# Recurrent attention and gated feed-forward on one Trainium2 core: normalisation steps spread over the score pass, norms stored ahead of the row maxima

## The reference

```python
x = L0_attn_x
xn = _layernorm(x, axis=-1)
s = _L0_attn_ref(xn, L0_attn_Wq, L0_attn_Wk, L0_attn_Wv, L0_attn_Wo)
g = _silu(_L0_ffn_ref(xn, L0_ffn_w_fc, L0_ffn_w_proj))
x = x + s * g
...
scores = jnp.einsum('bhqd,bhkd->bhqk', q, k) / math.sqrt(dk)
scores = jnp.where(causal[None, None], scores, -jnp.inf)
attn = jax.nn.softmax(scores, axis=-1)
```

## Time and profile before

| what | value |
|---|---|
| time, median of 3 runs | 1205.97 us (1204.27 to 1207.26) |
| profiled execution, its time | 1208.05 us |
| profiled execution, its span | 1206.2 us |
| TensorE busy | 1157.1 us, 96% of the span |
| VectorE busy | 851.2 us, 71% |
| ScalarE busy | 787.0 us, 65% |
| GpSimd busy | 522.0 us, 43% |
| mean granted TensorE clock | 0.995 |

### The profile page before, as it was taken

The page is one execution under the profiler, slowest core; times in us unless marked ns, Lnnn a source line. Parts: engine busy times, 40 slices in busy tenths (PEclk is TensorE's granted clock), DMA queues, the critical chain, the costliest instruction groups (busy, mean ns, idle before and its releaser), DMA issues.

```text
span 1206.2 us, 19952 instructions
## 1 busy us (share of the span) xinstructions
PE 1157.1 (96%) x7580; PEld 562.3 (47%) x7580; DVE 851.2 (71%) x1445; ACT 787.0 (65%) x1486; POOL 522.0 (43%) x894
## 2 busy tenths in 40 slices
PE   4989999999999999999899999999989999999997
PEld 3555544445444454445444454444534445444553
DVE  7988948697457975588446985569735797557864
ACT  3687974487825977269561797438873487816974
POOL 2135361463525544363343635246352463526434
PEclk9999999999999999999899999999999999999999
DMA  8390011900137000550007401091011900146010
GB/s 296 149 117 26 1 28 50 161 19 2 28 39 136 19 4 26 78 115 1 26 4 85 108 2 29 1 155 38 3 28 17 158 19 2 27 55 95 9 38 36
DMA packets 52537, 67.30 MB, mean 56 GB/s; under 512 B 9304, under 2 KB 34264, under 8 KB 51928
## 3 DMA queue, kind: packets, MB, share of 16 engines
q1 hardware_dynamic: 52440, 66.01, 29.0%
HBM read 31.98 MB, written 8.40 MB: 33 GB/s over the span
## 4 chain that ended last, share of the span: by engine, by line
PE 60%; DVE 20%; ACT 15%; DMA 3%; issue 1%; SPq 1%; DVEq 0%; ACTq 0%
PE banks L378 24%; PE banks L524 9%; PE banks L493 9%; ACT banks L778 8%; PE banks L609 5%; PE banks L578 5%; DVE mix L1025 4%; ACT arena L799 4%; DVE arena L1049 4%; DVE arena L1047 4%; PE banks L472 2%; DMA stacks<-mix 2%; DVE banks L1033 1%; PE banks L399 1%; DVE mix L1039 1%; DVE mix L928 1%
## 5 line engine op out<-in xcount | busy, mean ns | idle before, releaser
L524 PE MATMUL banks<-projT,arena 128*128 128x512 f16 x1024 | 293.7, 380 | 0.0
L778 ACT ACTIVATE banks<-banks,mix,scl 128x512 f32<-128x512 f32 (+2 forms) x384 | 250.1, 698 | 4.5 <-POOL mix L1218 2.2
L1025 DVE TENSOR_REDUCE mix<-banks 128x1 f32<-128x384 f32 (+3 forms) x352 | 221.1, 639 | 28.7 <-PE banks L479 15.6
L493 PE MATMUL banks<-xT,fcT 128*128 128x512 f16 x1024 | 227.7, 379 | 0.1
L799 ACT ACTIVATE arena<-banks,scl 128x1280 f32<-128x1280 f32 x128 | 164.7, 1328 | 72.4 <-PE banks L578 69.3
L1211 POOL TENSOR_TENSOR xh_buf<-xh_buf 128x512 f32<-128x512 f32 x120 | 152.3, 1269 | 90.7 <-ACT xh_buf L747 86.5
L1202 POOL TENSOR_TENSOR split_buf<-xr_buf,split_buf 128x512 f16<-128x512 f32 x64 | 74.0, 1178 | 238.8 <-ACT split_buf L724 238.8
L378 PE MATMUL banks<-xT,qkT 128*128 128x512 f16 x768 | 168.7, 379 | 0.0
L1218 POOL TENSOR_SCALAR mix<-mix,scl 128x1 f32<-128x1 f32 (+1 forms) x288 | 76.3, 265 | 182.9 <-DVE mix L1025 182.3
L493 PEld LDWEIGHTS banks<-xT,fcT 128*128 128x128 f16 x1024 | 97.7, 98 | 120.1 <-ACT xh_buf L747 8.0
L1232 POOL TENSOR_SCALAR_AFFINE_SELECT arena<-arena 128x256 f32<-128x256 f32 x256 | 102.7, 428 | 90.0 <-ACT arena L799 90.0
(11 more groups left out here) (148 smaller groups left out, 1563.7 us busy)
## 6 DMA issues: line engine op xcount, KB each, us to landing
stacks<-split_buf SPq DMA_DIRECT2D x192, 128.0 KB, 5.5
xr_buf<-in_L_attn_x_dram SPq DMA_DIRECT2D x8, 1024.0 KB, 7.6
out_dram<-arena SPq DMA_DIRECT2D x32, 256.0 KB, 2.3
resid<-in_L_attn_x_dram SPq DMA_DIRECT2D x28, 256.0 KB, 6.8
stacks<-in_L_ffn_w_fc_dram SPq DMA_DIRECT2D x1, 4096.0 KB, 27.1
arena<-in_L_ffn_w_proj_dram SPq DMA_DIRECT2D x1, 4096.0 KB, 14.6
mix<-norm_row SPq DMA_DIRECT2D x8, 256.0 KB, 4.6
v_sb<-in_L_attn_Wv_dram SPq DMA_DIRECT2D x1, 1024.0 KB, 8.2
```

Of the source, the lines that this page charges most:

```text
L493: mm = pe.matmul(banks[:, UP_BANKS[f % NUB], :], fcT[:, c, f * P:(f + 1) * P], xT[:, part, c, :], start=(c == 0 and part == 0), stop=(c == ...
L524: mm = pe.matmul(banks[:, 6 + t % 2, :], lhs, projT[:, f, :], **ends)
L778: mm = nc.scalar.activation(block, block, ACT.Exp, scale=col(EXP_SCALE), bias=exp_bias[:, i, h0 + k:h0 + k + 1], accum_out=row_sum[:, i, h ...
L1025: nc.vector.tensor_reduce(row_max[:, i, h0:h0 + n], scores_of(r), AX_X, ALU.max).then_inc(max_ready, 1)
```

## The change

GpSimd's `normalise` becomes a generator, `normalise_steps`, that pauses after each of its ten operations. In the first score pass one operation is issued ahead of each bias from round 8 on, so they stand ahead of the biases of rounds 8 to 17. The operations themselves and their semaphores are the same. Of SyncE's `spread_norms` the four norm stores become a function of their own, `store_norms`, and are written ahead of the wait for `maxT_ready`, so ahead of the maxima transfer. The read back stays behind it.

```diff
+NORM_FROM = 8
...
+            def store_norms(b):
+
+                sp.wait_ge(ln_ready, b + 1)
+                for t in range(NT):
+                    sp.dma_start(norm_row[t * P:(t + 1) * P], norm_c[:, t:t + 1]).then_inc(row_dma, 16)
+
             def spread_norms(b, first=False):
 
-                sp.wait_ge(ln_ready, b + 1)
-                for t in range(NT):
-                    sp.dma_start(norm_row[t * P:(t + 1) * P], norm_c[:, t:t + 1]).then_inc(row_dma, 16)
                 sp.wait_ge(row_dma, b * NT * 16 + NT * 16)
...
+                if not last:
+                    store_norms(b + 1)
                 sp.wait_ge(maxT_ready, b + 1)
                 sp.dma_start(q_stack[KS:KM, :, :], maxT[:, :]).then_inc(max_dma, 16)
                 if not last:
                     spread_norms(b + 1)
 
+            store_norms(0)
             spread_norms(0, first=True)
...
+                steps = normalise_steps(b + 1)
                 for r in LONG[BIAS_DVE:]:
                     i, h0, n = ROUNDS[r]
+                    if r >= NORM_FROM and not last:
+                        next(steps, None)
                     pool.wait_ge(max_ready, b * NR + r + 1)
...
-                if not last:
-                    normalise(b + 1)
```

More of the change, by code:

```diff
@@ L271, in store_result @@
                         load_resid(b, t + 2)
-            def spread_norms(b, first=False):
+            def store_norms(b):
                 sp.wait_ge(ln_ready, b + 1)
@@ L277, in spread_norms @@
                     sp.dma_start(norm_row[t * P:(t + 1) * P], norm_c[:, t:t + 1]).then_inc(row_dma, 16)
+            def spread_norms(b, first=False):
                 sp.wait_ge(row_dma, b * NT * 16 + NT * 16)
@@ L1166, in _, with normalise_steps @@
             LN_STEPS = 9
-            def normalise(b, first=False):
+            def normalise_steps(b, first=False):
                 mean, var = mean_var[:, :, 0], mean_var[:, :, 1]
@@ L1181, in normalise @@
                 step(1, nc.gpsimd.tensor_scalar(a1, var, LN_EPS, None, ALU.add))
+                yield
                 step(2, nc.gpsimd.tensor_tensor(r1, a1, minus_half[:], ALU.pow))
+                yield
                 step(3, nc.gpsimd.tensor_tensor(sq, r1, r1, ALU.mult))
+                yield
                 step(4, nc.gpsimd.tensor_tensor(v2, sq, var, ALU.mult))
+                yield
                 step(5, nc.gpsimd.tensor_scalar(a2, v2, BIT_EPS, None, ALU.add))
+                yield
                 step(6, nc.gpsimd.tensor_tensor(r2, a2, minus_half[:], ALU.pow))
+                yield
                 step(7, nc.gpsimd.tensor_tensor(rr, r1, r2, ALU.mult))
+                yield
                 step(8, nc.gpsimd.tensor_tensor(shift, mean, rr, ALU.mult))
+                yield
                 step(9, nc.gpsimd.tensor_tensor(norm_c[:], a2, r2, ALU.mult))
+                yield
                 nc.gpsimd.tensor_scalar(shift, shift, -1.0, None, ALU.mult).then_inc(ln_ready, 1)
+                yield
+            def normalise(b, first=False):
+                for _ in normalise_steps(b, first):
+                    pass
             def add_x(b, t):
```

## The result

The changed kernel takes 1194.93 us (median of 4 runs, 1194.36 to 1195.38). The kernel before took 1205.12 us beside it (median of 4, 1203.73 to 1207.26). The ratio is 0.9912, with a 95% interval of 0.9886 to 0.9937. The prediction was 1194.5 us, with a range of 1191 to 1200. The span of the profiled execution is 1193.4 us, against 1206.2 before.

The account below looks back on a forecast made before the run. The chain ran through TensorE (60%), VectorE and ScalarE (35%), and 2% a late maxima transfer. On the profiled execution 1208.05 - 13.65 + 0.3 = 1194.7 us; predicted 1194.5, range 1191 to 1200.

Parts of the forecast that it names:

- The late landings are the cost: Maxima transfer before the second score pass: late in images 1, 3 and 5, costing 13.65 us against 8.9 us of waits.
- the half clock: TensorE after a stall of over 3 us: paid a second time at half clock, 3.1 us in image 3.
- The norm stores behind the transfer cause them: SyncE: four norm stores about 1.0 us behind the maxima transfer sometimes hold up its end; moving them saves 13.65 us.
- The slowest landings of the kernel: Norm stores on SyncE: claimed to land slowest, 6.6 us at the median for 0.5 KB.
- The rule that spoke against the change: Maxima transfer: only earlier writes of the same DMA engine delay the semaphore, so moving the norm stores would save nothing.
- this rival: Late landings don't come from the norm stores, since what is issued behind may not hold: 1204 to 1208 us, chance 8%.
- The moved operations at 0 at the end of the pass: GpSimd's ten operations taken off the end of the first score pass: not waited for there, so 0 gained.
- The bias of round 13 late by 1.05 us, with a margin of 0.15: GpSimd, first score pass: second power makes this bias 1.05 us late, under 1.20 us of slack, so ScalarE doesn't see it.
- Image 0 pays 0.3 us: Round 9 of image 0: slack only 0.56 us, so the power delays ScalarE by 0.2 to 0.6 us, taken as 0.3.
- The base of the unprofiled runs: Other runs, median 1205.97 us, carry most of the stalls: 1192.6 us if the same; with fewer, the profile's floor.

Follow-up runs that it names:

- the control: The kernel with GpSimd's part alone, plus the spare tensor in memory and one tiny store issued behind the last output store: 1223.77 us, ratio 1.0112.
- GpSimd's part alone: The changed kernel with the norm stores put back behind the maxima transfer: 1216.19 us, ratio 1.0067.
- the order on SyncE alone: The kernel before with the norm stores ahead of the maxima transfer and GpSimd untouched: 1259.42 us, ratio 1.0423.

## Why the prediction was right

- *The late landings are the cost, and they are worth more than the waits show.* Right, in kind and in size: 13.65 us were expected and 13.8 came back, with the half clock gone as well. Both are of the two profiled executions.
- *The norm stores behind the transfer cause them.* Right as far as it goes. Two pairs of kernels with the same order on SyncE show it: with the stores some 1.0 us behind the transfer three images are late, held back until it has landed none; with the stores 1.8 us ahead seven are late, 26 us ahead none. Adding tiny stores brings late transfers back, even in image 7. What the prediction left out is that stores behind the transfer need a second condition. It said "sometimes"; the profile of the kernel before is late in images 1, 3 and 5 and in no other, and one or two stores issued once, over 200 us earlier, take that away while the norm stores stay where they were. I read it as depending on how many transfers SyncE has issued before, which the expectations call the place in the DMA rings. Apart from the extra tensor, which the control rules out, these kernels changed nothing else ahead of the transfer than one or two issues. That it is a place in the rings, and what it is about it, wasn't seen. By luck the forecast didn't depend on it: without tiny stores to memory in flight beside the transfer nothing was late in any kernel, whatever had been issued before.
- *"The slowest landings of the kernel".* Not so. The same list of DMA issues has larger loads that land later, up to 27.1 us for 4 MB, and three transfers of 16 KB (`stacks<-ones`) with 8.7 us. The norm stores are the slowest stores to memory, 6.6 against 2.3 us. Nothing in the sum rests on it.
- *The rule that spoke against the change.* "DMA: Bandwidth & Descriptors", section "Queues, rings and completion order", in the Trainium skill has the increment wait for every earlier write of its DMA engine. The run with the stores ahead of the transfer agrees: all seven transfers landed late, 7.0 to 8.5 us after their issue. But the rule alone gives no late transfer for stores that are issued behind, and there were three in the kernel before and three in the run with tiny stores added. The measurement decides: this rival, with its 8%, didn't come true.
- *The moved operations at 0 at the end of the pass.* Right: GpSimd's part alone gains nothing. It even loses some 8 us against the kernel before (1216.19 against 1207.79), late in the same images but by more. The stores follow 0.2 us closer there; that this is the reason was not tested by itself. The prediction didn't see that, and in the full change it doesn't matter.
- *The bias of round 13 late by 1.05 us, with a margin of 0.15.* The term was mis-sized, on the safe side. Timelines of the changed kernel in image 1's round 13:

```profile
269.63 0.27 POOL L1242 TENSOR_SCALAR mix<-mix,scl 128x1 f32<-128x1 f32 x1
...
270.44 0.81 ACT L785 ACTIVATE banks<-banks,mix,scl 128x512 f32<-128x512 f32 x1
```

The bias is ready at 269.90, 0.54 us before it is used, where it was 1.28 before, so it is 0.74 late and not 1.05. From one bias to the next with a light operation between it is 0.51 to 0.55 us, once 0.67, and not 0.26 + 0.36 = 0.62 or more; with a power it is 1.37 and not 0.26 + 1.20 = 1.46. In most of these pairs the operation starts 0.22 us after the start of the bias, which is recorded with 0.27.

- *Image 0 pays 0.3 us.* Right. In its round 9 the power reaches ScalarE, whose exponential starts 0.91 us after the one before (122.86) instead of 0.76; with a smaller gap in round 13 it is about 0.25 us in all:

```profile
122.33 1.04 POOL L1190 TENSOR_TENSOR ln<-ln,minus_half 128x4 f32<-128x4 f32 x1
123.47 0.27 POOL L1242 TENSOR_SCALAR mix<-mix,scl 128x1 f32<-128x1 f32 x1
```

```profile
123.77 0.75 ACT L785 ACTIVATE banks<-banks,mix,scl 128x512 f32<-128x512 f32 x1
```

The span fell by 12.8 us, not by 13.8 - 0.25 = 13.55. The rest, 0.7 us, is lost before image 0's first score pass, which starts at 105.94 before and at 106.60 after. It is lost at the very start, where the same sixteen matmuls take 2.38 us before and 3.40 after:

```profile
21.95 2.38 PE L399 MATMUL banks<-ident,xh_buf 128*128 128x128 f32 x16
```

```profile
21.71 3.40 PE L406 MATMUL banks<-ident,xh_buf 128*128 128x128 f32 x16
```

The change touches nothing ahead of them. In the other runs the first score pass starts between 105.35 and 106.39 us with no pattern that follows an edit, so I count it as play of the start; why these matmuls were slower wasn't looked into.

- *The base of the unprofiled runs.* The prediction assumed that they carry most of the stalls, and chose 1194.5 between 1192.6 and 1194.7. The kernels without a late image take 1194.1 to 1195.0 us, and the changed kernel's own 1194.93 lies 10.2 us under the median beside it, 1205.12. So the time was that of a kernel without stalls, and the gain less than the 13.35 us of the profiled execution, which was slower than that median.

## What to carry to other kernels

A DMA that an engine waits for shouldn't have tiny writes to memory in flight beside it, neither ahead nor right behind it: issue them long before, or wait for the landing first, which cost nothing here. A lucky number of earlier transfers hides the loss, but the next edit can bring it back. Before crediting a gain to a rearranged kernel, compare the same transfer over all iterations; if it is late in a fixed pattern, add one harmless transfer early in the program and see whether the pattern moves. A stall of TensorE can cost more than its length: the stalls of 3.3 to 6.4 us behind late stores lost 1.3 to 1.8 times as much, with a stretch at half clock behind them (3.8 us of waiting, 6.88 lost), and the one of 1.8 us lost nothing more.

## What the runs showed that I had not expected

- One store of 512 bytes, issued once in image 0, moves the kernel before from medians of 1205 to 1210 us to 1194.09, and the kernel with GpSimd's part alone from 1216.19 to 1195.86.
- Fractions of a microsecond at the issue seem to matter: with the stores 0.83 us behind the maxima transfer it took 8.6 to 9.0 us in the late images, with 1.03 us 5.5 to 7.5. Each is from one profile.
- The half clock may begin inside the idle gap. In the kernel with the order on SyncE alone TensorE is idle for 7.48 us up to 619.44 in image 3, and over 614.70 to 618.40, inside this gap, the granted clock is already 0.51:

```profile
614.70:618.40 3.70, 0.00 (x0) 0.00 (x0) 0.76 (x2) 0.00 (x0) 0.00 (x0) 0.51 0.00 0
```

```profile
619.44 0.91 PE L584 MATMUL banks<-stacks 99*128 99x512 f16 x2 [7.48 <-DMA stacks<-mix]
```
